# The mixer's two input projections as three float32r products each, with the gate computed half a sequence ahead

## The reference

```python
proj = jnp.einsum('bsd,ed->bse', x, in_proj_w)
gate = proj[..., :INTER]                       # INTER = 128 heads x 64
hBC  = proj[..., INTER:INTER + CONV_DIM]       # values, B, C
dt   = proj[..., INTER + CONV_DIM:]
hBC  = silu(depthwise causal conv of hBC, 4 taps)
...                                            # chunked scan over chunks of 128 tokens: Y
y = Y.reshape(b, s, INTER)
g = y * jax.nn.silu(gate)
gg = g.reshape(b, s, G, INTER // G)            # G = 8 groups of 1024 channels
gg = gg * rsqrt(mean(gg * gg, -1) + EPS)
return einsum('bsi,oi->bso', gg * norm_w, out_proj_w)
```

## Time and profile before

| | |
|---|---|
| median of 3 runs | 2969.13 us (2967.29 to 2969.56) |
| the profiled execution | 2967.0 us, its span 2965.2 us |
| mixer with its preparation | about 0 to 2099 us of the span |
| busy, share of the span | PE 2758.0 (93%), DVE 1940.1 (65%), ACT 1129.7 (38%), POOL 593.5 (20%) |
| conv steps on DVE, L741 | mean 0.880 us of 480, least 0.742 |
| median time from issue to landing of a DMA | a conv tile's weights (256 KB) 2.7 us; half a row of `EC` (256 KB) 8.3 us; the gate's or the output's weights of a group (2 MB) 8.1 and 8.9 us |
| granted TensorE clock | 0.971 mean; 0.7 in the first two of 40 slices, then 0.9 or more in nearly all |

### The profile page before, as it was taken

How to read it: one execution, slowest core, us unless ns; L and a number is a source line. 1 busy time by engine, 2 the same in 40 slices (tenths; PEclk the granted TensorE clock), 3 DMA queues, 4 the chain that set the end, 5 groups by cost and what they waited for, 6 DMA issues and landing times. The chain is left out here.

```text
span 2965.2 us, 42961 instructions
## 1 busy us (share of the span) xinstructions
PE 2758.0 (93%) x15936; PEld 1805.8 (61%) x15936; DVE 1940.1 (65%) x3087; ACT 1129.7 (38%) x2241; POOL 593.5 (20%) x512
## 2 busy tenths in 40 slices
PE   3699999999999999999999999999698889999899
PEld 2266666666766666666676666667586444444388
DVE  5566777677677677767767767775554646666364
ACT  1333434344343343434434334342221336666421
POOL 1222132221213213222121321222221001111031
PEclk7799999999999999999999999999798989999999
DMA  4211121121112212112211212301101401111000
GB/s 147 62 35 39 46 88 38 43 91 44 37 59 73 39 46 88 38 42 92 44 38 60 72 38 47 88 20 23 75 0 74 164 29 40 38 38 36 1 11 18
DMA packets 128562, 155.94 MB, mean 53 GB/s; under 512 B 29344, under 2 KB 89840, under 8 KB 125680
## 3 DMA queue, kind: packets, MB, share of 16 engines
q1 hardware_dynamic: 122912, 151.34, 18.0%
q10 hardware_dynamic: 5456, 2.00, 0.3%
HBM read 134.93 MB, written 18.38 MB: 52 GB/s over the span
## 5 line engine op out<-in xcount | busy, mean ns | idle before, releaser
L455 PE MATMUL bank<-xnT,wh 128*128 128x512 f32 x1280 | 573.7, 599 | 29.4 <-issue 26.2
L741 DVE SCALAR_TENSOR_TENSOR cacc<-raw,cwh,cacc 128x512 f32<-128x512 f32 x480 | 421.8, 880 | 221.4 <-ACT cacc L726 210.0
L549 PE MATMUL bank<-xnT,wg 128*128 128x128 f32 x4096 | 480.1, 275 | 0.0
L549 PEld LDWEIGHTS bank<-xnT,wg 128*128 128x128 f32 x4096 | 467.3, 192 | 3.3 <-issue 3.3
L592 PE MATMUL bank<-wo,yt 128*128 128x512 f32 x1024 | 453.0, 595 | 7.9 <-DVE yt L839 7.9
L455 PEld LDWEIGHTS bank<-xnT,wh 128*128 128x128 f32 x1280 | 236.7, 191 | 296.7 <-issue 288.5
L592 PEld LDWEIGHTS bank<-wo,yt 128*128 128x128 f32 x1024 | 193.6, 190 | 247.6 <-issue 247.6
L651 ACT COPY xs<-bank 128x512 f32<-128x512 f32 x128 | 74.5, 582 | 414.7 <-PE bank L481 414.7
L1981 DVE TENSOR_REDUCE at_nm<-bank 128x1 f32<-128x512 f32 (+3 forms) x256 | 150.3, 589 | 109.3 <-PE bank L1847 89.2
L934 POOL TENSOR_TENSOR rr<-rr,nhalf 128x1 f32<-128x1 f32 x64 | 35.2, 549 | 914.0 <-DVE rr L872 914.0
L1945 ACT ACTIVATE at_PT<-bank 128x512 f32<-128x512 f32 (+3 forms) x384 | 167.4, 498 | 118.2 <-PE bank L1860 114.0
(11 more groups left out here) (240 smaller groups left out, 4393.5 us busy)
## 6 DMA issues: line engine op xcount, KB each, us to landing
wh<-w_hs_dram SPq DMA_DIRECT2D x160, 256.0 KB, 2.7
EC<-ecum_scratch SPq DMA_DIRECT2D x112, 256.0 KB, 8.3
wg<-w_gate_dram SPq DMA_DIRECT2D x8, 2048.0 KB, 8.1
wo<-w_out_dram SPq DMA_DIRECT2D x8, 2048.0 KB, 8.9
qk_scratch<-at_part SPq DMA_DIRECT2D x48, 256.0 KB
at_qT<-qk_scratch SPq DMA_DIRECT2D x32, 192.0 KB, 2.6
at_kT<-qk_scratch SPq DMA_DIRECT2D x32, 192.0 KB, 2.7
wgu<-w_gu_dram SPq DMA_DIRECT2D x1, 3584.0 KB, 11.2
```

Of the source, the lines that this page charges most:

```text
L455: mm = nc.tensor.matmul(BA[bank][:, :], wh[:, i % WR, k, :], xnT[:, k, h * HALF:(h + 1) * HALF], start=(k == 0), stop=(k == KC - 1))
L549: mm = nc.tensor.matmul(BA[b][:, i * P:(i + 1) * P], wg[:, k, j * P:(j + 1) * P], xnT[:, k, ttok], start=(k == 0), stop=(k == KC - 1))
L741: nc.vector.scalar_tensor_tensor(dst, raw[:, r, 2 - k:2 - k + HALF], w(2 - k), dst, ALU.mult, ALU.add)\
```

## The change

Every projection tile, conv or gate, becomes 12 float32r matmuls of 512 columns: high weights times high input, high times low, low times high. The input is split once, before the slots (`xh` by ACT, `xl` by POOL). The weights are split tile by tile: SP loads a tile into one of three raw buffers (two of them the old `xn`), ACT copies it to float32r (`ac_high`, placed behind the copy or the gate tanh of the tile three before), POOL subtracts (`po_low`), and PE waits for that.

The gate is no longer made in the slot that uses it. A gate tile is 128 channels by 512 tokens, made with the conv tiles of the half ahead: two in each slot, eight in the prologue, none in the last four slots. Its product goes to `G2`, where a finished block of the one half is replaced by one of the other half (`gate_tile`, `gate_chunk`). The multiplication of `yt` moves up on DVE, behind L805. The 2 MB load of a group's gate weights and its wait are gone. The second state buffer `st1` is gone, so POOL's multiplication waits for PE's two readings of the state; the square is written over `xs`.

```diff
@@ -147,29 +147,46 @@
+        RR, WR = 3, 3
+        ORDER = [JB, JC] + list(range(JT))
+        SHARE = [(0, 4), (4, 7), (7, 10), (10, 10)]
+        TILES = [t for c, (lo, hi) in enumerate(SHARE)
+                 for t in [("gate", 2 * c), ("gate", 2 * c + 1)] + [("conv", i) for i in range(lo, hi)]]
+        NTILE = len(TILES)
+        STEPS = 2 * G
+        LAST_TILE = STEPS * NTILE
+        xh = sb(ctx, "xh", [P, KC, T], F32R)
+        xl = sb(ctx, "xl", [P, KC, T], F32R)
+        rawx = sb(ctx, "rawx", [P, KC, P])
+        wh = sb(ctx, "wh", [P, WR, KC, P], F32R)
+        wl = sb(ctx, "wl", [P, WR, KC, P], F32R)
+        raws = [rawx[:, :, :]] + [xn[:, r, :].rearrange("p (k m) -> p k m", k=KC) for r in range(2)]
+        d_raw = [sem(ctx, f"d_raw{j}") for j in range(RR)]
+        wo_set = sem(ctx, "wo_set")
...
+        def number(p, kind, i):
+            return (2 * p[0] + p[1]) * NTILE + TILES.index((kind, i))
+        def load_tile(sp, q):
+            if q >= LAST_TILE:
+                return
+            g, (kind, i) = q // (2 * NTILE), TILES[q % NTILE]
+            if kind == "conv":
+                src = A["w_hs"][bass.ds(g, 1), :, ORDER[i]]
+            else:
+                src = A["w_gate"][bass.ds(g, 1), :, :, i * P:(i + 1) * P]
+            sp.dma_start(raws[q % RR], src.rearrange("o p k m -> p (o k) m")).then_inc(d_raw[q % RR], 16)
...
                         act.wait_ge(ln_ps, z + 1)
-                        nc.scalar.copy(xnT[:, :, z * P:(z + 1) * P],
-                                       BANK[z % 2][:, :].rearrange("p (k t) -> p k t", k=KC)).then_inc(ln_xt, 1)
+                        for dst in (xnT, xh):
+                            nc.scalar.copy(dst[:, :, z * P:(z + 1) * P],
+                                           BANK[z % 2][:, :].rearrange("p (k t) -> p k t", k=KC)).then_inc(ln_xt, 1)
...
+                    for z in range(NT):
+                        cols = slice(z * P, (z + 1) * P)
+                        pool.wait_ge(ln_xt, 2 * (z + 1))
+                        nc.gpsimd.tensor_tensor(xl[:, :, cols], xnT[:, :, cols], xh[:, :, cols], ALU.subtract).then_inc(p_ch, 1)
...
-        def pe_tile(pe, p, i, bank):
-            j = ORDER[i]
-            h = p[1]
-            step = 2 * p[0] + h
-            pe.wait_ge(d_wh[i % WR], 16 * (2 * step + i // WR + 1))
+        def gates_done(n, u):
+            return JT + 2 * n + u + 1
+        def gate_tile(p, j):
+            a, b = j // 2, j % 2
+            return G2[:, a, b, :, :] if p[1] == 0 else G2[:, :, b, a, :]
+        def gate_chunk(h, c):
+            if h == 0:
+                return G2[:, :, :, c, :].rearrange("p a b t -> p (a b) t")
+            return G2[:, c, :, :, :].rearrange("p b a t -> p a b t")
+        def pe_tile(pe, p, kind, i, bank):
+            q = number(p, kind, i)
+            s, tok = q % WR, slice(p[1] * HALF, (p[1] + 1) * HALF)
+            po_lo.wait(pe, q + 1)
             for k in range(KC):
-                mm = nc.tensor.matmul(BA[bank][:, :], wh[:, i % WR, k, :], xnT[:, k, h * HALF:(h + 1) * HALF],
-                                      start=(k == 0), stop=(k == KC - 1))
+                for m, (w, x) in enumerate(((wh, xh), (wh, xl), (wl, xh))):
+                    mm = nc.tensor.matmul(BA[bank][:, :], w[:, s, k, :], x[:, k, tok],
+                                          start=(k == 0 and m == 0), stop=(k == KC - 1 and m == 2))
             mm.then_inc(pe_P.sem, 1)
...
-            pe.wait_ge(d_wg, 16 * g + 16)
             for u in range(2):
-                release_a(pe, g, z, u)
-                b = bank()
-                for i in range(4):
-                    j = 4 * u + i
-                    for k in range(KC):
-                        mm = nc.tensor.matmul(BA[b][:, i * P:(i + 1) * P], wg[:, k, j * P:(j + 1) * P], xnT[:, k, ttok],
-                                              start=(k == 0), stop=(k == KC - 1))
-                mm.then_inc(pe_gt.sem, 1)
+                if step:
+                    release_a(pe, g, z, u)
+                    pe_tile(pe, step, "gate", 2 * (z % CH) + u, bank())
                 if mine and u == 0 and not last:
                     pe_hidden(pe, *nxt, 1)
...
                 if r < 2:
-                    dv_sg.wait(pe, 2 * n + r + 1)
+                    dv_sg.wait(pe, gates_done(n, r))
                 else:
                     ac_raw.wait(pe, RAW * ((2 * step[0] + step[1]) * PT + mine[r] - 1))
-                pe_tile(pe, step, mine[r], bank())
+                pe_tile(pe, step, "conv", mine[r], bank())
...
+            elif step:
+                dv_sg.wait(pe, gates_done(n, 0))
             else:
-                dv_sg.wait(pe, 2 * n + 1)
+                dv_sg.wait(pe, STEPS * JT)
+                dv_out.wait(pe, n - 1)
...
+        def ac_high(act, q):
+            if q >= LAST_TILE:
+                return
+            act.wait_ge(d_raw[q % RR], 16 * (q // RR + 1))
+            pe_P.wait(act, q - WR + 1)
+            nc.scalar.copy(wh[:, q % WR, :, :], raws[q % RR]).then_inc(ac_hi.sem, 1)
+        def ac_gate_tanh(act, p, j, bank):
+            q = number(p, "gate", j)
+            m = (2 * p[0] + p[1]) * JT + j
+            dv_sg.wait(act, m - 1)
+            pe_P.wait(act, q + 1)
+            nc.scalar.activation(sg[:, j % 2 * 512:(j % 2 + 1) * 512], BA[bank][:, :], ACT.Tanh, scale=0.5)\
+                .then_inc(ac_tg.sem, 1)
+            ac_high(act, q + WR)
         def ac_xs_copy(act, g, z, u):
             n = 8 * g + z
             dv_xc.wait(act, n)
+            dv_sq.wait(act, n - 1)
             pe_hs.wait(act, 2 * n + u + 1)
             nc.scalar.copy(xs[:, u * 512:(u + 1) * 512], BT[1 - u][:, :]).then_inc(ac_xs.sem, 1)
...
-                dv_gg.wait(act, n)
-                pe_gt.wait(act, 2 * n + u + 1)
-                nc.scalar.activation(sg[:, u * 512:(u + 1) * 512], BA[bank()][:, :], ACT.Tanh, scale=0.5)\
-                    .then_inc(ac_tg.sem, 1)
+                if step:
+                    ac_gate_tanh(act, step, 2 * (z % CH) + u, bank())
...
             dv_gg.wait(act, n + 1)
             dv_sq.wait(act, n)
+            if not last:
+                dv_xc.wait(act, n + 2)
             nc.scalar.activation(sq, yt[:, :], ACT.Square).then_inc(ac_sq.sem, 1)
...
+            ac_high(act, q + WR)
...
+        def dv_gate_tile(dve, p, j, bank, gated):
+            m = (2 * p[0] + p[1]) * JT + j
+            ac_tg.wait(dve, m + 1)
+            dv_gg.wait(dve, gated)
+            t3 = lambda ap: ap.rearrange("p (c t) -> p c t", c=CH)
+            nc.vector.scalar_tensor_tensor(gate_tile(p, j), t3(sg[:, j % 2 * 512:(j % 2 + 1) * 512]), 1.0,
+                                           t3(BA[bank][:, :]), ALU.add, ALU.mult).then_inc(dv_sg.sem, 1)
...
+            dv_yd.wait(dve, 2 * n + 2)
+            dv_sg.wait(dve, (n // CH + 1) * JT)
+            shape = "p (j t) -> p j t" if h == 0 else "p (a b t) -> p a b t"
+            yv = yt[:, :].rearrange(shape, t=P, **({"j": JT} if h == 0 else {"a": 4}))
+            nc.vector.tensor_tensor(yv, yv, gate_chunk(h, c), ALU.mult).then_inc(dv_gg.sem, 1)
...
-                            nc.vector.tensor_tensor(st[:, cols], st1[:, cols], BY[u][:, :], ALU.add).then_inc(dv_st.sem, 1)
+                            nc.vector.tensor_tensor(st[:, cols], st[:, cols], BY[u][:, :], ALU.add).then_inc(dv_st.sem, 1)
...
             for u in range(2):
-                su = sg[:, u * 512:(u + 1) * 512]
-                ac_tg.wait(dve, 2 * n + u + 1)
-                nc.vector.scalar_tensor_tensor(su, su, 1.0, BA[bank()][:, :], ALU.add, ALU.mult).then_inc(dv_sg.sem, 1)
+                if step:
+                    dv_gate_tile(dve, step, 2 * (z % CH) + u, bank(), n + 1)
-            dv_yd.wait(dve, 2 * n + 2)
-            dv_sg.wait(dve, 2 * n + 2)
-            nc.vector.tensor_tensor(yt[:, :], yt[:, :], sg[:, :], ALU.mult).then_inc(dv_gg.sem, 1)
...
+        def po_low(pool, q):
+            if q >= LAST_TILE:
+                return
+            ac_hi.wait(pool, q + 1)
+            pe_P.wait(pool, q - WR + 1)
+            nc.gpsimd.tensor_tensor(wl[:, q % WR, :, :], raws[q % RR], wh[:, q % WR, :, :], ALU.subtract).then_inc(po_lo.sem, 1)
...
             if 0 < z < NT - 1:
                 dv_st.wait(pool, skip_last(g, z, 2))
-                nc.gpsimd.tensor_tensor(headed(st1[:, :]), headed(st[:, :]), per_head(h, c, O_LAST), ALU.mult)\
+                pe_yo.wait(pool, skip_first(g, z, 2) + 2)
+                nc.gpsimd.tensor_tensor(headed(st[:, :]), headed(st[:, :]), per_head(h, c, O_LAST), ALU.mult)\
                     .then_inc(po_s1.sem, 1)
+            if step:
+                for u in range(2):
+                    po_low(pool, number(step, "gate", 2 * (z % CH) + u) + WR)
...
             if not last:
                 po_pre(pool, *nxt)
+            for i in mine:
+                po_low(pool, number(step, "conv", i) + WR)
...
+                def next_tile(q):
```

(27 more changed lines are left out.)

88 lines of the change are left out of this document (34 added, 54 removed).

## The result

The changed kernel takes 3034.63 us (median of 4 runs, 3029.15 to 3038.59) against 2968.64 before (2967.29 to 2969.56): 1.0221 times as long, 95% interval 1.0204 to 1.0239, 66 us slower. The profiled execution (3029.15, the fastest of the four) has a span of 3027.4 (before 2965.2); the rows of the changed kernel are from it. The difference lies in the mixer alone: its last sum of squares starts at 2159.5 instead of 2097.5, 62.0 later, and what follows lasts 867.9 (867.7 before).

A forecast was written before the change was run, and what follows sets the result against it. PE and the ACT/DVE chain were taken to end a slot nearly together. Seven full groups +7.7, half the eighth +4.0, prologue +24 and end -29 made +7 on 2967.0, hence 2976 us; range 2845 to 3045.

The forecast's parts named there:

- rival (b): In the groups' slots: each subtraction holds DVE for its full 1.28 us, giving 3052 us; chance 0.20.
- My sign for (b): In the trace: slots with three conv tiles near 34 us would point to subtractions holding DVE their full 1.28.
- The matmuls: On PE: float32r matmuls start 0.228 us apart, saving 0.69 a conv tile and 0.74 a gate tile.
- The hold of 0.9: On DVE: a POOL subtraction falling among conv steps costs DVE about 0.9 us (bounds 0 and 1.28).
- z=0, z=4, z=3 and z=7: Slots by chunk number: +4.6 us through POOL's queue, -2.3 with four convs, 0 for the two without convs.
- Prologue and last four slots: Prologue, making 18 tiles in place of 10: +24 us; last four slots, losing their gate tiles: -29 us.
- Slots with three convs: z=1, 2, 5, 6: -0.3 us each; PE ready 1.4 earlier, first conv tile 0.4 later, awaiting the gate product.
- Rival (a): In the groups: PE stays the bound, subtractions meeting idle DVE or its PSUM steps; 2836 us, chance 0.28.
- my list of what would make the prediction wrong: In the trace: three-conv slots near 30 or 34, PE waiting on raw tiles' loads, another clock in the groups.

The follow-up runs named there:

- no_sub: Changed kernel with POOL's weight subtraction cut to 8 of 512 columns from the fourth tile on, stale low weights multiplied instead: 2822.64 us.
- z0_order: Changed kernel with POOL's order in z=0 alone altered: second-half taps, first gate subtraction, output-weight scaling, second gate subtraction: 3011.69 us.
- filler: Changed kernel with eight matmuls of zeros on PE ahead of the first conv tile of slots with three conv tiles: 2999.51 us.
- filler_all: Changed kernel with zero matmuls also in PE's pauses in z=0, before sums of squares in slots with conv tiles, and in the prologue: 2992.62 us.
- f32_ahead: Changed kernel without the split: tiles multiplied in float32 from the raw buffers, the gate still made half a sequence ahead: 2937.97 us.
- late_all: Changed kernel with subtractions moved behind gate or masked products, z=3 and z=7 included, z=0 reordered on POOL, prologue copies before the preceding tanh: 2824.34 us.
- late_conv: Changed kernel with only the conv tiles' last three subtractions waiting for the masked products, the last behind the power: 2950.59 us.
- late: Changed kernel, in slots with conv tiles: gate subtractions wait for DVE's second gate product (not in z=0), the last three conv ones for masked products: 2874.78 us.

## Why the prediction was right or wrong

The forecast was 2976, the measurement 3034.6: slower, inside the range, but 59 above the value that I called likeliest and near rival (b), 3052, whose mechanism didn't happen. My sign for (b), slots with three convs near 34, came true by another cause, so that sign could not tell the two apart. Step by step:

- **The matmuls**: right. 0.228 between starts at full clock, 16 in 3.3 us.
- **The hold of 0.9**: right. Three conv steps that took 2.33 take 3.24 in the new prologue with one subtraction among them:

```profile
114.50 3.24 DVE L790 SCALAR_TENSOR_TENSOR cacc<-raw,cwh,cacc 128x512 f32<-128x512 f32 x3 [1.41 <-ACT cacc L774]
115.05 1.36 POOL L960 TENSOR_TENSOR wl<-xn,wh 128x512 fp32r<-128x512 f32 x1 [3.90 <-ACT wh L682]
```

That is 0.91; over all 285 it is 0.77 (no_sub). The mean of L741's successor came out at 1.012, not 1.1 to 1.2, because I had put too many of the holds on the conv steps: the silu and `xch` took their share. Rival (b), the full 1.28, is refuted by the same rows. Its sum was also off: 6.3 + 4 x 1.2 - 0.9 is 10.2 a group and not 10.7, about 3048 in all.

- **z=0, z=4, z=3 and z=7**: +4.5, -2.1, -0.2 and -0.2 against +4.6, -2.3, 0 and 0. Right, with the waits named (above, z0_order).
- **Prologue and last four slots**: +27.6 and -27.7 against +24 and -29. Mechanisms right, sizes off by 3.6 and 1.3. The last slot took 14.9, not 13.1, and that is the clock again: it has a low stretch, and in the runs in which it has none (filler, filler_all, f32_ahead) it takes 13.2.
- **Slots with three convs**: here it failed. The forecast put PE at the first conv tile at 13.3 and the gate product at 15.1; the rows show 13.4 and 15.3. At full clock such a slot is 32.74, 0.05 below before (-0.3 forecast). But the step took PE's 1.8 us of idleness as free, with the clock left as it was. The clock fell in 22 of the 30 slots, in 19 of them behind that pause, in the others around the slot's start, and the mean of all 30 is 34.29: (34.29 - 32.74) x 30 = 46.5 of the 55 us by which the mixer exceeds the forecast in the trace; the 0.25 a slot between -0.05 and -0.3 is another 7.5. The clock stood last in my list of what would make the prediction wrong, without a price; it was the largest term of the sum that I had left out.
- **Rival (a)**: 2836 for the case that nothing holds DVE. Its condition wasn't met by the change, but its size was about right: 2822.6 with the subtraction cut, 2824.3 with it moved (late_all, which also has z=0's new order and the prologue's step).

What stays open: which of two equal pauses is followed by a fall (the twin slots of groups 3 and 4). The rows show that it happens, not by what it is decided. What the extra ACT copies cost isn't shown either, beyond the 0.8 a slot that bounds it (no_sub). And late_conv has z=4 at 31.6, where late has 32.2: leaving that slot's gate subtractions in their old place would perhaps gain a little more; it wasn't tried.

## What to carry to other kernels

Work put on an idle engine isn't free: look at which steps of other engines its instructions hold up, and put it beside steps that aren't held, here those that read PSUM or reduce; the subtractions cost 212 us where the change put them, and with nearly all of them moved a slot with three convs took 30.17, against 30.03 with them cut. When an engine gets faster than its supplier, price the new pause as well: a TensorE pause of 2 us in a dense stream can cost 1.6 more through the clock, and filling it with idle products is a quick test of that. Move both of two holds that end in the same place before judging either; one alone only moved the pause.
